# Decoder layer on one core: score and exponential tiles in groups of two, three stacks, a stage order for each engine, whole-array mask products

## The reference, cut to what matters

```python
x = x + rbf_attention(layernorm(x))                    # 8 batches of 256 tokens, width 256
x = x + cross_attention(ctx, ctx, layernorm(x), mask)  # 16 heads of 16 columns
x = x + top2_of_8_experts(layernorm(x))                # hidden width 1024

# rbf_attention:   scores = exp(-(|q|^2 + |k|^2 - 2 q.k));  softmax(scores) @ v @ Wo
# cross_attention: energy = q_h @ k_h.T for each head, masked;  softmax(energy / 4) @ v_h, then @ Wo
# experts:         gate = xs @ Wg;  the two best experts of a token, relu(x W1 + b1) W2 + b2, weighted
```

## Time and profile before

| | |
|---|---|
| Time, median of 3 runs | 639.74 us (638.13 to 639.81) |
| The profiled execution: its own time | 636.72 us |
| Its span, first to last instruction | 635.0 us |
| PE busy | 577.4 us, 91% |
| DVE busy | 364.6 us, 57% |
| ACT busy | 330.5 us, 52% |
| POOL busy | 219.2 us, 35% |
| Mean granted TensorE clock | 0.966 of full |

### The profile page before, as it was taken

The page is one execution under the profiler, slowest core; times in us unless marked ns, Lnnn a source line. Parts: engine busy times, 40 slices in busy tenths (PEclk is TensorE's granted clock), DMA queues, the critical chain, the costliest instruction groups (busy, mean ns, idle before and its releaser), DMA issues.

```text
span 635.0 us, 15573 instructions
## 1 busy us (share of the span) xinstructions
PE 577.4 (91%) x5107; PEld 492.0 (77%) x5108; DVE 364.6 (57%) x856; ACT 330.5 (52%) x723; POOL 219.2 (35%) x285
## 2 busy tenths in 40 slices
PE   3878799999999999998967889999999999999992
PEld 3765667677686776756445889999999999999992
DVE  3547666768677777856878786574232332323321
ACT  4533365564647456452445674555656556565560
POOL 5322212212313121111013616533554555545542
PEclk9859999999999999998979799999999999999996
DMA  8483909064270907346159955766666675666841
GB/s 226 117 98 88 117 3 108 12 79 76 41 111 2 151 4 91 63 57 96 35 187 322 297 170 167 185 195 200 174 208 204 186 219 174 213 198 186 222 99 17
DMA packets 55880, 85.67 MB, mean 135 GB/s; under 512 B 6576, under 2 KB 44592, under 8 KB 55824
## 3 DMA queue, kind: packets, MB, share of 16 engines
q1 hardware_dynamic: 46368, 73.59, 47.8%
q0 software_dynamic: 7744, 10.29, 8.5%
q10 hardware_dynamic: 1712, 1.05, 0.6%
HBM read 62.44 MB, written 9.31 MB: 113 GB/s over the span
## 4 chain that ended last, share of the span: by engine, by line
PE 76%; DVE 7%; DMA 5%; ACT 4%; issue 3%; POOL 2%; SPq 1%; ACTq 0%; POOLq 0%; DVEq 0%
PE pair L2105 21%; PE bank L2145 17%; PE bank L1020 16%; PE pair L1262 5%; PE bank L1374 4%; PE pair L1284 3%; PE pair L1342 3%; PE bank L986 2%; PE bank L2069 1%; ACT exp_ring L1356 1%; DMA q_stack<-cq_lo 1%; DMA slots_in<-xn_rows,gather_now 1%; DMA experts_w<-L_ffn_W 1%; DVE tr_lo L1010 1%; DVE tile_vals L1848 1%
## 5 line engine op out<-in xcount | busy, mean ns | idle before, releaser
L2105 PE MATMUL pair<-slots_t,w_now 128*128 128x128 f32 x1248 | 146.9, 276 | 0.3 <-DMA w_now<-L_ffn_W 0.3
L2105 PEld LDWEIGHTS pair<-slots_t,w_now 128*128 128x128 f32 x1248 | 143.6, 193 | 0.5 <-DMA w_now<-L_ffn_W 0.5
L2115 ACT ACTIVATE hid<-pair,b_tile 128x128 f32<-128x128 f32 x312 | 88.9, 367 | 54.7 <-PE pair L2105 54.7
L2125 DVE TENSOR_TENSOR hid_lo<-hid,hid_hi 128x1024 fp32r<-128x1024 f32 x39 | 47.8, 1226 | 107.2 <-ACT hid_hi L2122 107.2
L2058 POOL DMA_INDIRECT out<-y,scatter_now x39 | 64.0, 1640 | 115.3 <-DMA out<-y,scatter_now 76.9
L1293 DVE TENSOR_REDUCE row_max<-pair 128x4 f32<-128x1024 f32 x64 | 77.1, 1218 | 10.6 <-PE pair L1284 10.6
L2145 PE MATMUL bank<-experts_w,hid_hi 128*128 x624 | 83.1, 285 | 0.0
L1356 ACT ACTIVATE exp_ring<-pair 128x1024 f32<-128x1024 f32 x64 | 63.8, 1024 | 33.3 <-PE pair L1342 32.2
L2145 PEld LDWEIGHTS bank<-experts_w,hid_hi 128*128 128x128 f32 x624 | 76.2, 188 | 0.0
L2043 POOL DMA_INDIRECT slots_in<-xn_rows,gather_now x39 | 43.4, 1112 | 25.8 <-POOL gather_now L2040 15.4
L2122 ACT ACTIVATE hid_hi<-hid 128x512 fp32r<-128x512 f32 x78 | 49.4, 633 | 4.7
(11 more groups left out here) (279 smaller groups left out, 1080.8 us busy)
## 6 DMA issues: line engine op xcount, KB each, us to landing
w_now<-L_ffn_W SPq DMA_DIRECT2D x39, 1024.0 KB, 5.1
experts_w<-L_ffn_W SPq DMA_DIRECT2D x8, 1024.0 KB, 7.0
k_stack<-ck_hi SPq DMA_DIRECT2D x32, 128.0 KB, 4.2
q_stack<-cq_hi SPq DMA_DIRECT2D x32, 128.0 KB, 6.2
ctx_in<-ctx SPq DMA_DIRECT2D x8, 256.0 KB, 7.5
k_stack<-ck_lo SPq DMA_DIRECT2D x16, 128.0 KB, 5.6
q_stack<-cq_lo SPq DMA_DIRECT2D x16, 128.0 KB, 7.5
out<-x SPq DMA_DIRECT2D x7, 256.0 KB, 7.4
```

Of the source, the lines that this page charges most:

```text
L2105: mm = eng.matmul(banks[half][:, f * P:(f + 1) * P], core.w1_now[b.p][:, c, start:start + P], core.slots_t[b.p][:, c, :], start=c == 0, st ...
L2115: act = eng.activation(core.hid[:, g, :], banks[half][:, f * P:(f + 1) * P], ACT.Relu, bias=core.b1_tile[b.p][:, g:g + 1])
```

## The change

- `mask_product` writes the mask of a bank with one matmul over the whole 128 x 128 identity, 512 columns wide: two matmuls for a tile and no swapped masks. Their DMAs at the start are gone.
- PE takes tiles in groups (`quad`): the masks of exponential tile i (batch n-2) and of score tile i (batch n-1), then the products of both.
- From batch 1 on, score tiles use `pair[1]` alone; exponential tiles use `pair[0]` alone, except those of the last batch.
- There are three stacks (`STACKS`), by batch modulo 3.
- Each engine has a stage order of its own. `st_heads_transposed` and "hT" move from lag 2 to lag 3.
- `st_project`, `st_output` and `st_rbf_out` do the products with hi parts first and wait for the lo part only before the rest.

```diff
-def mask_product(core, eng, pair, mask, turned):
-    for c, part in enumerate((mask, turned)):
-        for r in range(2):
-            left = slice(r * HALF, (r + 1) * HALF)
-            to = left if c == 0 else slice((1 - r) * HALF, (2 - r) * HALF)
-            eng.matmul(pair[to, c * 512:(c + 1) * 512], core.ident_bf[left, left], part[left, :, :],
-                       start=True, stop=False, skip_group_check=True)
+def mask_product(core, eng, pair, mask):
+    for c in range(KT):
+        eng.matmul(pair[:, c * 512:(c + 1) * 512], core.ident_bf[:, :], mask[:, :, :],
+                   start=True, stop=False, skip_group_check=True)
+def scores_pair(core, b, i):
+    return core.pair[1 if b.v > 0 else i % 2]
+def exps_pair(core, b, i):
+    return core.pair[0 if b.v < NB - 1 else i % 2]
+def scores_open(core, name, eng, b, it, i):
...
+    if b.v == 0:
+        core.e["maxed"].wait(eng, b if i >= 2 else b.back(1), i - 2)
+    elif i == 0:
+        core.e["maxed"].wait(eng, b.back(1))
+    else:
+        core.e["maxed"].wait(eng, b, i - 1)
+    mask_product(core, eng, scores_pair(core, b, i), core.mask_q)
+def exps_open(core, name, eng, b, it, i):
+    if i == 0:
+        core.m["stacked"].wait(eng, b)
...
+    elif i >= 1:
+        core.e["exp"].wait(eng, b, i - 1)
...
+    mask_product(core, eng, exps_pair(core, b, i), core.mask_k)
+def quad(at, i):
+    at(2, exps_open, i)
+    at(1, scores_open, i)
+    at(2, exps_products, i)
+    at(1, scores_products, i)
+def attention_tensor(core, eng, it):
...
+        at(0, st_rbf)
+    at(3, st_heads_transposed)
+    quad(at, 0)
+    at(0, st_transpose, "ctxT")
+    at(0, st_rbf_out)
+    quad(at, 1)
+    if choosing:
+        prefix_product(core, eng, 0)
+    at(0, st_project, "ck")
+    at(3, st_transpose, "hT")
+    quad(at, 2)
+    at(2, st_weighted, 0)
+    if placing:
+        table_product(core, eng, 0, 0)
+    at(3, st_output)
+    at(0, st_transpose, "xcT")
+    quad(at, 3)
...
+    at(0, st_project, "cq")
+    at(-1, st_transpose, "xnT")
+    quad(at, 4)
+    at(2, st_weighted, 1)
...
+    quad(at, 5)
+    at(-1, st_project, "k")
+    at(3, st_router_transpose)
+    quad(at, 6)
+    at(2, st_weighted, 2)
...
+    at(3, st_router)
+    at(-1, st_project, "q")
+    at(-1, st_key_norms)
+    quad(at, 7)
+    at(-1, st_value)
+    at(2, st_weighted, 3)
+    at(1, st_maxima)
+    at(0, st_cross_value)
+    if placing:
+        at(2, st_heads_transposed)
+        at(2, st_transpose, "hT")
+def attention_scalar(core, eng, it):
...
+    at(2, st_weighted, 3)
+    at(1, st_maxima)
...
+    elif choosing:
+        split_expert(core, "scalar", eng, 1)
+        split_expert(core, "scalar", eng, 2)
+def attention_vector(core, eng, it):
...
+    at(0, st_moments, 1)
...
+    at(3, st_transpose, "hT")
+    at(0, st_project, "ck")
+    at(0, st_normalise, 1)
+    at(1, st_scores, 2)
...
+    at(1, st_scores, 3)
+    at(3, st_moments, 2)
+    at(0, st_project, "cq")
+    if choosing:
+        routing_counts(core, eng, 0)
+        first_tiles(core, eng)
...
+    at(1, st_scores, 4)
...
+def attention_sync(core, eng, it):
...
+    if it.v == NB:
+        core.e["t_tile"].wait(eng, LAST_BATCH.back(2))
+        load_expert(core, eng, 1)
...
+    at(1, st_maxima)
+    if it.v == NB:
+        core.e["t_tile"].wait(eng, LAST_BATCH.back(1))
+        load_expert(core, eng, 2)
```

More of the change, by code:

```diff
@@ L38 @@
 PAIRS = H // KT
+STACKS = 3
 VCOLS = D + 2
@@ L586, in setup_stacks @@
     E = core.E
-    for p in range(2):
+    for p in range(STACKS):
         for c in range(KT):
@@ L729, in at @@
             fn(core, name, eng, b, it, *args)
[L731 to L763, removed]
+    return at
@@ new lines, in attention_sync @@
+def attention_sync(core, eng, it):
+    at = stages(core, "sync", eng, it)
+    if it.v == -1:
+        at(-1, st_normalise, 0)
+        setup_constants(core, eng)
+        core.e["p_q"].wait(eng, it.back(-1))
+        rows = core.t["x"].rearrange("b (t p) d -> p (b t) d", p=P)
+        loads(core, eng, core.x2[:, 2 * KT:, :], rows[:, 2 * KT:, :], core.E["x_rest"])
+        return
+    if it.v == 1:
+        for x in range(EARLY):
+            load_expert(core, eng, x)
+    if it.v == NB:
+        core.e["t_tile"].wait(eng, LAST_BATCH.back(2))
+        load_expert(core, eng, 1)
+    at(-1, st_normalise, 0)
+    at(0, st_project, "ck")
+    at(3, st_output)
+    at(0, st_project, "cq")
+    at(3, st_normalise, 2)
+    at(1, st_maxima)
+    if it.v == NB:
+        core.e["t_tile"].wait(eng, LAST_BATCH.back(1))
+        load_expert(core, eng, 2)
+        experts_sync(core, eng)
+    elif it.v == NB + 1:
+        experts_rest_sync(core, eng)
@@ new lines, in scores_products @@
+def scores_products(core, name, eng, b, it, i):
+    q_stack, k_stack, pair = core.q_stack[b.v % STACKS], core.k_stack[b.v % STACKS], scores_pair(core, b, i)
+    for qt in range(KT):
+        for c in range(KT):
+            rows = slice(c * HALF, c * HALF + QROWS)
+            mm = eng.matmul(pair[:, c * 512 + qt * S:c * 512 + (qt + 1) * S],
+                            q_stack[rows, i, qt * P:(qt + 1) * P], k_stack[rows, i, :],
+                            start=False, stop=True, skip_group_check=True)
+    core.e["s_tile"].at(mm)
@@ L1298, in st_maxima @@
+def st_scores(core, name, eng, b, it, i):
+    pair = scores_pair(core, b, i)
+    if i == 0:
+        core.e["p_max"].wait(eng, b.back(1))
+    core.e["s_tile"].wait(eng, b, i)
+    maxima = core.row_max[:, :, :].rearrange("p t (c i) -> p c t i", c=KT)[:, :, :, i]
+    core.e["maxed"].at(eng.tensor_reduce(maxima, pair[:, :].rearrange("p (c t k) -> p c t k", c=KT, t=KT),
+                                         AX.X, ALU.max))
 def st_maxima(core, name, eng, b, it):
```

492 lines of the change are left out of this document (237 added, 255 removed).

## The result

The changed kernel takes 658.06 us (median of 4, 655.63 to 663.28), the kernel before 638.93: ratio 1.0317, 95% interval 1.0263 to 1.0370. It is 19 us slower. The forecast was 656.5.

What follows compares the result with a forecast made beforehand. PE's work was taken to bound steady iterations, so its waits add in full. Start -3.2, intervals +2.7, it 8 +9.9 and it 9 +7.4 sum to +16.8 on 636.72, 653.5; the median stands 3.0 above: 656.5, range 644 to 664.

Steps and rivals of the forecast that it cites:

- The start: Up to the maxima of it 1: hi products first and moved stages shorten waits for lo parts, -3.2 us.
- A group: Masks and products of two tiles in steady iterations: 1.68 us; PE's work 35.3 to 35.6 or 36.1 an iteration, 36.1 taken.
- and the rest gives back about that: Steady iteration: masks take 1.8 us more (0.91 for 0.68 a group), fewer changes of shape return about as much.
- The stack wait: Each iteration, between maxima transposes and group 0: stack ready after 5.37, PE's work lasts 4.4, so about 1.0 us idle.
- Intervals: Six intervals from the first maxima to those of it 7: 214.9 against 212.1 us, +2.7.
- It 8: Routing counts on DVE hold up group 5, after other waits: 38.5 us between transposes where it was 28.65, +9.9.
- (c): Rival: new idle stretches in it 8 and 9 each bring a half-speed stretch, +2 to +3 each; 663 us, chance 0.13.
- It 9: Expert 2's load and rounding delay batch 7's exponentials to 12.0 after the transposes; last table product ends +7.4 us later.
- Had 1.5 of slack: After it 9's last table product: heads' transposes come 8.9 later, but had 1.5 us of slack against the gathers.
- (a): Rival: the steady part gains, intervals of 34.5 to 35.4 us if change-overs saved give back the load; 644 us, chance 0.12.
- (b): Rival: kernel gets faster, PE's work in an interval under 33, steady interval under 33.7 us; 636 us, chance 0.07.
- (d): Rival: the ends hurt only half as much, as the expert tiles' start absorbs part; +8, 648 us, chance 0.13.

Runs made afterwards that it cites:

- hi first alone: Kernel before, with only st_project and st_output doing hi-part products first and waiting for the lo part later: 639.1 us, ratio 0.998.
- quarter masks: Changed kernel with each mask product again four quarter-array matmuls side by side, swapped masks and their DMAs back: 641.0 us, ratio 1.004.
- the first experiment: Changed kernel with the wait for the stack moved behind the first group's mask products, ahead of the products only: 647.8 us, ratio 1.015.
- counts late: Changed kernel with all of it 8's routing counts on DVE but three copies moved behind the maxima: 651.7 us, ratio 1.019.
- split late: Changed kernel with ACT rounding the second expert matrix behind exponential tile 3 of batch 7, not ahead of tile 0: 652.5 us, ratio 1.021.
- the fillers: Changed kernel plus repeated, useless mask products in PE's idle rows of it 8 and it 9: 654.8 us, ratio 1.023.
- the three repairs: Changed kernel with stack wait behind the first masks, rest of the routing counts behind the maxima, second expert matrix rounded behind exponential tile 3: 642.3 us, ratio 1.003.

## Why the forecast was right, and where it was not

The forecast named the right mechanisms: whole masks cost more array time than the changes of shape give back, and three new waits stand in PE's way. The sizes were off in both directions, and the nearness of the total (656.5, measured 658.1) owes something to chance: the steady part was forecast too dear by 3.9 (the chance fall in it 6 left out), it 8 too cheap by 5.8, and the 4.4 ahead of the first expert tile was not in the sum.

**The start** (-3.2, measured -2.9). Its parts are found: the wait ahead of "xcT" is 2.57 (forecast 2.65), those ahead of "cq" and "k" 0.78 and 0.99 for 1.50 and 1.68. That these parts make the sum was only argued; the run with hi first alone shows no more than 0.4, and no run has the new order of the start alone.

**A group** (1.68, measured 1.62; PE's work 36.1, measured 35.2). The step that was mis-sized is "and the rest gives back about that". With quarter masks an iteration is 36.4 - 33.8 = 2.6 shorter, the stack wait included, and whole masks take 2.5 of it (forecast 1.8). How much of the 2.6 is the grouping and how much the stages' new order was not separated. I had taken the upper of my two counts; the lower bound, 35.3, was near. The quarter blocks of two tiles, which I had at 0.68, take 0.56 when they stand together (182.70 to 183.26), and the four whole matmuls 0.95, so the masks take 0.39 more in each group and not 0.23. By the first half of the Trainium skill's rule ("TensorEngine Tiling (Array Packing)", Key Properties) whole masks cost 1.8 more; the trace agrees, since the quarter matmuls of a block start 0.01 apart and a block of them takes about the time of one whole matmul (182.70 to 182.94). The second half says that a change of mode drains the engine. The 0.10 ahead of a quarter block fits that, though the trace shows a delay and not its reason; it gives back only 0.8 of 3.1 in eight groups. The sum goes against whole masks in groups and in single tiles alike.

**The stack wait** (1.0, measured 0.83; transposes to mask 5.37 forecast, 5.35 measured). Right. What I did not see is that the masks don't need the stack: they could stand ahead of the wait, which the first experiment did.

**Intervals** (+2.7, measured +3.6 in the profiled execution). The agreement is by chance: it is -1.2 without the fall in it 6. There, PE went on 7.3 us after the transposes and not 5.35, and the clock was at its lower level from 224 to 231. The profiles of counts late and split late show the same stretch late by 1.8 and 1.5 (it 6 is 39.6 and 39.3), that of the fillers, whose program is the same up to it 8 but for the order of two waits, does not. The trace shows where the time goes. ACT, DVE and the four issues on SP stand as far behind the transposes as in other iterations (the last issue 3.15); of the last one's 16 packets two start late, at 223.6, and PE's semaphore is complete 6.81 behind the transposes where it is 5.07 elsewhere. From 222.4 to 223.6 a fetch of 16 KB of instructions is under way. The DMA packets from 222.35 to 222.50 show its one packet, and those from 223.55 to 223.90 the two late ones:

```profile
q8 instruction: 1, 0.02, 51.1%
q1 hardware_dynamic: 2, 0.00, 2.9%
```

In all three late cases the two packets start within 0.02 of the end of such a fetch, which began 4.41 to 4.44 behind the transposes; in the fillers' it 6 it began at 6.01 and nothing was late. A fetch that began at 4.49 in it 4 of the three repairs held nothing up, so that the fetch is the cause is argued from the times and not shown.

**It 8** (+9.9, measured +15.7). The chain is as forecast: idle rows of 2.2, 2.2 and 5.4 in the three places (forecast 2.8, 2.6, 5.8). The missing 5.8 I put down to the clock, which the forecast had put into rival (c) with 2 to 3 for each stretch: a mean of 0.77 over 44.3 us is 20 us at half. The fillers show some 4.0 of it (one execution of each; 3.3 in the medians), with one slow stretch still left; the rest was argued from the granted clock. The Trainium skill ("TensorE: Matmul & The Clock Gate", HAM oscillation) says that the cost is paid each time; the trace agrees, with stretches at the lower level from 296 to 310 and from 324 to 331 in it 8 and from 337 to 351 in it 9. The forecast and (c) are not alternatives; (c) belonged into the sum.

**It 9** (+7.4, measured +7.1). The number is right and the step named is real: the split late takes 4.2 of it away. But the exponentials started 10.9 behind the transposes and not 12.0, while a mean clock of 0.71 (16 of 27.9 us at half) was not in the sum, so the two errors offset each other.

**Behind the last table product** (0, measured +4.4). "Had 1.5 of slack" was wrong, since it looked at the gathers (they are issued from 368.9 on and land within 5 us, while PE comes to the first expert tile at 378.34). In the new order exponential tile 7, the last sum, the heads, "hT" and the output product of batch 7 all stand behind that table product, each waiting for the one before: four idle rows, 3.6 us together, the work between them at half clock. In the kernel before tile 7 stood ahead of it. The error is in where I let the sum end: at an event and not at PE's next stage.

**Rivals.** (a) and (b) fall by the interval of 36.25. (b)'s mechanism exists, though: without whole masks the interval is 33.8, with the masks ahead of the wait 33.2, under the 33.7 that was its point of decision, and the kernels with it are at 635.9 and 626.3. (d) falls: the expert tiles give back 1.2, and the ends cost more than forecast.

## What to carry to other kernels

Matmuls that use a quarter of the array side by side should not be merged into whole ones to save changes of shape, unless the change costs as much as the array time they share; here it was 0.1 against 0.4. A wait belongs ahead of the first instruction that needs its data, not ahead of the group: writing the masks first was worth 10 us in the changed kernel and 5 with quarter masks. And when a new order moves long small work of another engine, price the idle row that it leaves on TensorE with the slow stretch behind it, and follow the sum to the next engine that waits.

## What was not expected of the hardware

Waits of 0.83 in each steady iteration left the clock at its upper level. It went to the lower one during waits of 2.2 to 5.4 us (it 6, twice in it 8), and in it 9 behind two waits of 0.87 and 1.10 close together; it stayed there for up to 13.6 us, although PE was at work for most of these. Running 30 useless matmuls in it 8's waits (6.8 us at the upper level) made that stretch 4.0 us shorter. And in it 6 of three profiled executions the landing of a small DMA was 1.5 to 1.8 us late, just when a fetch of instructions was under way.
